# Outputs turned in blocks on VectorE and spread by small DMAs, value products in groups of three key tiles, and a shorter last gate

## What is computed

```python
def _proj(x, w, b, n_head):                 # q, k and v: 8 heads of 16
    y = jax.nn.elu(_conv1d_valid(x, w) + b)
    ...
scores = jnp.einsum('bhqd,bhkd->bhqk', q, k) / jnp.sqrt(jnp.float32(dh))
attn = jax.nn.softmax(scores, axis=-1)
out = jnp.einsum('bhqk,bhkd->bhqd', attn, v)
...
h = _L0_tok_ref(x, ...)
h = h + _L0_attn_ref(_layernorm(h, axis=-1), ...)   # gated unit, one head of 16, causal, gelu
h = h + _L0_ffn_ref(_layernorm(h, axis=-1), ...)    # router with 64 experts, top 2, capacity 128;
                                                    # all experts share w1, b1, w2, b2
```

## Time and profile before

| | us |
|---|---|
| median of 3 runs (824.22 to 829.16) | 825.8 |
| the profiled execution, by its own time | 826.22 |
| its span, from the first to the last instruction | 824.3 |
| PE busy | 793.2 |
| DVE busy | 673.1 |
| ACT busy | 519.8 |
| POOL busy | 259.4 |
| PE's first matmul of the second half, from the start | 538.4 |

### The profile page before, as it was taken

The page is one execution under the profiler, slowest core; times in us unless marked ns, Lnnn a source line. Parts: engine busy times, 40 slices in busy tenths (PEclk is TensorE's granted clock), DMA queues, the critical chain, the costliest instruction groups (busy, mean ns, idle before and its releaser), DMA issues. The chain is left out here.

```text
span 824.3 us, 15525 instructions
## 1 busy us (share of the span) xinstructions
PE 793.2 (96%) x5651; PEld 483.7 (59%) x5651; DVE 673.1 (82%) x1619; ACT 519.8 (63%) x1127; POOL 259.4 (31%) x253
## 2 busy tenths in 40 slices
PE   9799999999999999999999999979999999999996
PEld 5254454454454454454454444447778788787785
DVE  4788889889889889889888989458788887787855
ACT  4067776786786776787687777744645636546432
POOL 3563240350440341341332401314233242342222
PEclk9799999999999999999999999979999999999999
DMA  4462041042042034043032001000000000000001
GB/s 115 70 99 37 1 96 41 1 88 49 1 68 69 1 58 78 1 59 79 1 58 59 2 1 52 1 1 1 1 20 2 20 17 5 20 2 20 20 1 38
DMA packets 32427, 27.92 MB, mean 34 GB/s; under 512 B 5248, under 2 KB 31072, under 8 KB 32352
## 3 DMA queue, kind: packets, MB, share of 16 engines
q1 hardware_dynamic: 32112, 26.64, 16.3%
q10 hardware_dynamic: 240, 0.30, 0.2%
HBM read 4.76 MB, written 3.06 MB: 9 GB/s over the span
## 5 line engine op out<-in xcount | busy, mean ns | idle before, releaser
L429 ACT ACTIVATE probs<-ps_a 128x384 f32<-128x384 f32 (+1 forms) x732 | 299.7, 487 | 76.0 <-PE ps_a L625 71.1
L521 DVE TENSOR_REDUCE neg_max<-ps_a 128x1 f32<-128x512 f32 (+1 forms) x384 | 256.2, 683 | 56.2 <-PE ps_a L641 54.8
L625 PE MATMUL ps_a<-q_rep,k_rep 98*128 98x384 bf16 (+3 forms) x768 | 228.1, 323 | 1.3 <-DVE neg_max L523 1.2
L641 PE MATMUL ps_a<-k_rep,q_rep 96*128 96x512 bf16 (+3 forms) x768 | 219.2, 329 | 6.5 <-DVE neg_max L521 3.5
L641 PEld LDWEIGHTS ps_a<-k_rep,q_rep 96*128 96x128 bf16 (+1 forms) x768 | 76.7, 104 | 109.6 <-DVE neg_max L521 35.3
L656 PE MATMUL ps_pv<-probs,v_hat 128*32 128x364 f32 (+3 forms) x1536 | 140.6, 483 | 0.0
L523 DVE TENSOR_REDUCE neg_max<-ps_a 128x2 f32<-128x472 f32 x192 | 122.9, 640 | 0.0
L625 PEld LDWEIGHTS ps_a<-q_rep,k_rep 98*128 98x128 bf16 (+1 forms) x768 | 79.0, 104 | 58.2 <-ACT probs L429 30.5
L656 PEld LDWEIGHTS ps_pv<-probs,v_hat 128*32 128x32 f32 (+1 forms) x1536 | 40.1, 109 | 64.3 <-issue 58.5
L972 POOL TENSOR_SCALAR rs_v<-mv 128x6 f32<-128x6 f32 x8 | 2.0, 253 | 185.1 <-DVE mv L958 185.1
L258 POOL TENSOR_SCALAR qk_e<-qk_e 128x748 f32<-128x748 f32 x14 | 38.0, 2717 | 29.8 <-ACT qk_e L333 29.8
(11 more groups left out here) (222 smaller groups left out, 1203.0 us busy)
## 6 DMA issues: line engine op xcount, KB each, us to landing
q_rep<-parts_q SPq DMA_DIRECT2D x96, 96.0 KB, 3.8
k_rep<-parts_k SPq DMA_DIRECT2D x93, 96.0 KB, 3.6
xT<-in_x SPq DMA_DIRECT2D x8, 375.0 KB, 4.2
out_h<-y_out SPq DMA_DIRECT2D x7, 320.0 KB
q_rep<-max_T SPq DMA_DIRECT2D x32, 6.0 KB
w_sb<-in_w_T SPq DMA_DIRECT2D x2, 256.0 KB, 3.2
out_h<-y_out SPq DMA_DIRECT2D x8, 54.0 KB
k_rep<-parts_k ACTq DMA_DIRECT2D x3, 96.0 KB, 4.2
```

Source lines behind the costliest of these rows:

```text
L429: act.activation(probs[0:rows(kt), n % RING, 0:w], ps_a[0:rows(kt), 3 + n % 3, 0:w], ACT.Exp, scale=DH ** -0.5).then_inc(p_ready, 1)
L521: dve.tensor_reduce(neg_max[0:rows(t), 0, col:col + 1], ps_a[0:rows(t), c, :], AX.X, ALU.max, negate=True).then_inc(sc_max, 1)
L625: pe.matmul(out[0:rows(kt), 0:QW[qh]], k_rep[0:KM, cb % 2, h, kt * P:kt * P + rows(kt)], q_rep[0:KM, cb % 2, qh, h, 0:QW[qh]], start=True, ...
L641: last = pe.matmul(out, q_rep[0:KS, it % 2, t // QT, h, t % QT * P:t % QT * P + rows(t)], k_rep[0:KS, it % 2, h, 512:L] if c == 2 else k_r ...
```

## The change

- *Outputs.* `copy_output` and `turn_outputs` are gone. DVE's `outputs(cb, i)` turns a quarter straight out of `ps_pv`, in blocks of 32x32 (`dve.transpose`), and takes 12 reciprocals a partition; POOL's new `weigh_outputs` multiplies into `out_n`; SP's new `spread` sends them into `hall` by 16 DMAs for each half of the heads (each 32 partitions x 6 x 16 numbers). Semaphores `spread_done` take the place of `o_done` for those who read `hall`. The statistics of a batch and its `scales` come one iteration later.
- *Values.* `apply_pair` becomes `apply_group`: three key tiles in every third step. `even_step` and `odd_step` become `three_steps`.
- *Places.* What ACT and DVE do beside exponentials and reductions has new places, now given as (step, exponential) and (step, reduction).
- *The end.* For the last batch DVE makes the gates itself (`places_kept`, `gates_last`), the last Gelu comes in two halves, and the output is one fused instruction for a tile.

```diff
@@ first half, SP
+        def spread(cb, g):
+            sp.wait_ge(o_done, cb * 4 + 2 * g + 2)
+            for j in range(GH):
+                for c in range(P // 32):
+                    dst = hall[32 * c:32 * c + 32, cb * LP:(cb + 1) * LP].rearrange("p (t c) -> p t c", c=P)
+                    sp.dma_start(dst[:, :, GH * DH * g + DH * j:GH * DH * g + DH * j + DH],
+                                 out_n[32 * j:32 * j + 32, g, c:BLOCKS:P // 32, :]).then_inc(spread_done[g], 16)
...
                 maxima_rows(it - 1, 3)
+                spread(it - 1, 0)
...
             maxima_rows(it, 2)
+            if it > 0:
+                spread(it - 1, 1)
             if it == B - 1:
                 ahead["load"](sp)
         maxima_rows(B - 1, 3)
+        for g in range(NG):
+            spread(B - 1, g)
@@ first half, POOL
+        def weigh_outputs(cb, i):
+            k, u = cb * 4 + i, i % 2
+            pool.wait_ge(o_inv, k + 1)
...
+            pool.tensor_tensor(out_n[:, i // 2, nb * u:nb * u + nb, :], out_r[:, k % 2, :].rearrange("p (b d) -> p b d", d=32)[:, :, 0:DH],
+                               inv_sum[:, k % 2, :].unsqueeze(2).broadcast_to([P, nb, DH]), ALU.mult).then_inc(o_done, 1)
...
-                for w in "qk":
+            for i, w in enumerate("qk"):
+                if n < B:
                     negative(n, w)
                     residue(n, w)
+                if it > 0:
+                    weigh_outputs(it - 1, 2 + i)
+                if n < B:
                     third_part(n, w)
@@ first half, ACT
-                if s == 6:
-                    middle_part(n, "q")
...
-                if s == 6:
-                    exp_qk(n, "k")
...
+                if at == (5, 3):
+                    exp_qk(n, "k")
+                if at == (8, 0):
                     middle_part(n, "q")
@@ first half, DVE
-                if s == 9:
-                    elu_qk(n, "k")
...
+                if at == (8, 2):
+                    elu_qk(n, "k")
...
+            dve.transpose(out_r[:, k % 2, :], ps_pv[:, 0:QL]).then_inc(pv_copied, 1)
+            dve.wait_ge(pv_copied, k + 1)
+            dve.reciprocal(inv_sum[:, k % 2, :], out_r[:, k % 2, :].rearrange("p (b d) -> p b d", d=32)[:, :, DH]).then_inc(o_inv, 1)
...
+            if at in ((16, 0), (23, 0), (5, 0), (10, 0)):
+                i = ((16, 0), (23, 0), (5, 0), (10, 0)).index(at)
+                if i < 2 or it > 0:
+                    outputs(it - i // 2, i)
@@ first half, PE
+        def apply_group(it, s):
+            p = s - LAG - 3
             cb, cs = (it, p) if p >= 0 else (it - 1, p + STEPS)
...
+            if 0 <= cb < B and cs % 3 == 0:
+                for i in range(3):
+                    apply(cb, cs + i)
@@ second half, the last batch
+            if (n, f) == (B - 1, NF - 1):
+                for h in range(2):
+                    act.activation(hid[:, f, HALF * h:HALF * h + HALF], pair("ffn1", n, f)[:, h, 0:HALF], ACT.Gelu,
+                                   bias=b1_col[:, f:f + 1]).then_inc(S["z_hid"], 1)
...
+        def result_last(n, j):
+            transform(n, j)
+            dve.wait_ge(S["z_yb"], n * 3 + j + 1)
+            for t in range(*PARTS[j]):
+                dve.scalar_tensor_tensor(y_out[:, t, :], y_b[:, t, :], gate[:, t:t + 1], h2[:, n % 2, t, :],
+                                         ALU.mult, ALU.add).then_inc(S["z_out"], 1)
```

More of the change, by code:

```diff
@@ L430, in _ @@
                                            scale=DH ** -0.5).then_inc(p_ready, 1)
-                    if j == 1:
-                        between(it, s)
-                after(it, s)
-        ahead["bias_exp"](act, 1)
+                    after_exp(it, s, j)
         act.activation(warm[:, :], ident[:, 0:1], ACT.Gelu)
@@ L541, in before @@
                 maxima(it, s // 6 - 1)
-            if it == B and s == 0:
+            if at in ((16, 0), (23, 0), (5, 0), (10, 0)):
+                i = ((16, 0), (23, 0), (5, 0), (10, 0)).index(at)
+                if i < 2 or it > 0:
+                    outputs(it - i // 2, i)
+            if it == 0 and c == 1 and s in (2, 4):
+                elu_v(0, (s - 2) // 2)
+            if it > 1 and at in ((18, 0), (20, 2), (21, 0), (21, 1)):
+                part = ((18, 0), (20, 2), (21, 0), (21, 1)).index(at)
+                if part == 0:
+                    for done in spread_done:
+                        dve.wait_ge(done, SPREAD * (it - 1))
+                ahead["statistics"](dve, it - 2, plain_wait, part)
@@ L543, in before, with last @@
+            if it == 1 and at == (13, 0):
+                ahead["bias_sigmoid"](dve, 0)
+            if 2 <= it <= 5 and at in ((13, 0), (15, 0)):
+                ahead["bias_sigmoid"](dve, 2 * it - 3 + s // 15)
+        def last(s):
+            if s == 0:
+                maxima(B - 1, 3)
                 ahead["repeat_weights"](dve)
                 ahead["normalise"](dve, 0)
-            if it > 0 and s - 1 in turns(it):
-                k = turns(it).index(s - 1)
-                outputs(it - 1, k // 2, k % 2)
@@ L584, in _ @@
         copy_qk(1, 0)
-        for it in range(B + 1):
+        for it in range(B):
             for s in range(STEPS):
-                before(it, s)
-                if it < B:
-                    row_max(it, s, 0)
-                between(it, s)
-                if it < B:
-                    row_max(it, s, 1)
-                    row_max(it, s, 2)
+                for c in range(3):
+                    between(it, s, c)
+                    row_max(it, s, c)
+        for s in range(STEPS):
+            last(s)
     @block.tensor
@@ L1580, in _ @@
                     weigh(it, k)
-            if z:
+            if z and it < B:
                 transform(it - 1, 0)
             if it == 0:
+                for done in spread_done:
+                    dve.wait_ge(done, 16 * GH * (P // 32) * B)
                 G["statistics"](dve, B - 1, plain_wait)
@@ L1602, in _ @@
                 sum_2(it)
-        result_last(B - 1)
+        gates_last(B - 1)
+        for j in range(len(PARTS)):
+            result_last(B - 1, j)
     @block.tensor
```

279 lines of the change are left out of this document (138 added, 141 removed).

## The result

The changed kernel takes 868.2 us (median of 4 runs, 866.47 to 869.08) against 825.1 of the kernel before (median of 4). The two medians give a ratio of 1.052; the estimate from all runs is 1.050, with a 95% interval of 1.047 to 1.054. The forecast was 852 with a range up to 866: the sign was right, and the rise too small by 16 us. The profiled execution is the fastest of the four, 866.47 with a span of 864.7, so the spans differ by 40.4 and the medians by 43.1.

The account below looks back on a forecast made before the run. PE was taken to set each batch. Terms 0.5 (first batch) + 15.0 (six batches) + 1.3 (eighth) + 11.2 (boundary) + 1.5 (clock) - 3.1 (end) = +26.4 on 826.2: 852.6, median 852; range 838 to 866.

Parts of the forecast that it names:

- The order that goes wrong: Batches 2 to 7: q's late cast delays POOL's k negative part; DVE's maximum waits 4.4 us; +15.0 us in six.
- Rival 1: Batches 2 to 7: the wait for k's negative part doesn't appear, PE's saving stands; 826 or 819 us; chance 0.16.
- Between the halves: Token attention's end to second half: SP's 16 last transfers hold the barrier, the last group comes later; +11.2 us.
- The clock term: Behind the boundary: one more stretch at half clock after PE idles some 12 us; +1.5 us (0 to 3.4).
- PE's batch without the wait: Token attention, each batch: fewer turning matmuls and groups of three save PE 1.9 us, 63.2 to 61.3.
- The block transposes: DVE, four from PSUM in each batch: 0.55 us each, priced by the nearest PSUM read.
- rival 3: Unknown prices at upper ends, transposes 1.1 us and SP issues 1.26: 870 us and more; chance 0.11 shared with rival 4.
- The eighth batch: No convolutions beside it: groups of three leave DVE as the bound in all eight pieces, 54.5 against 53.2; +1.3 us.
- The end: Last batch: DVE makes gates while PE works, output is one fused instruction a tile; -3.1 us (-2 to -3.5).
- Rival 4: Groups of three starve DVE in batches with convolutions too: +4 us a batch, 875; chance 0.11 shared with rival 3.
- The first batch: Start of token attention: saves a little on PE, waits about 1 us in the same place; +0.5 us.

Follow-up runs that it names:

- pool_order: Changed kernel with POOL making k's negative part ahead of q's third part, ACT's cast of q's middle part staying late: 825.4 us, 0.999 of before.
- filler_17: Changed kernel with 17 useless identity matmuls on PE ahead of the waiting third score of step 9, batches 2 to 7: 853.5 us, 1.034 of before.
- pairs: pool_order with value groups of two key tiles in place of three, two of DVE's outputs also one step later: 854.1 us, 1.035 of before.
- tail_only: Kernel before with only the change's new end (last batch's gates, last Gelu, fused output): 821.3 us against 826.8, 0.994.
- cast_7_1: Changed kernel with ACT's cast of q's middle part moved earlier, behind the second exponential of step 7: 854.8 us, one run.
- cast_6_3: Changed kernel with ACT's cast of q's middle part moved earlier, behind the last exponential of step 6: 853.5 us, one run.
- before_cast_late: Kernel before with ACT's cast of q's middle part moved two steps later, from step 6 to step 8: 834.0 us, one run.
- deferred: pool_order with SP's last 16 transfers to hall issued behind the barrier, as its first work of the second half: 815.3 us, 0.986 of before.
- deferred_loads: deferred with the seven loads of second-half weights ahead of the 16 transfers after the last batch's third rows of maxima: 813.5 us, 0.984 of before.
- filler: Changed kernel with 34 useless identity matmuls on PE ahead of the waiting third score of step 9, batches 2 to 7: 875.1 us, 1.060 of before.

## Why the forecast was too low

**The order that goes wrong** was right in mechanism, place and size. DVE waits 4.6 us and PE 4.2 in each of six batches; the forecast had 4.4. Rival 1, that it doesn't appear, fell. Its upper value, 826, is what pool_order measures, where the cause was taken away.

**The step that failed** is the clock. The prediction gave it a term at one place, behind the boundary, by the earlier trace rows, and none in the six batches, although it forecast there a wait of PE of the same kind and of 4 us. That stretch of before came after four waits of PE of 0.65, 0.67, 0.82 and 1.05 us within ten microseconds (529.2 to 538.4), all shorter than the 4 us forecast for each batch. So the trace of before gave no reason to put the term at nothing there. The kernels pool_order, without the wait, and filler_17, with the wait filled, have no such stretch in their batches. The size: without the wait these six batches take 366.0 us (pool_order) in place of 377.1, -11.0; PE's idle adds 6 x 4.2 = 25.2; of the measured 29.2 that leaves 15.0 for the half clock. In a later batch that is 68.13 - 61.21 - 4.21 = 2.7, and the windows agree: PE works 5.42 us at 0.50, half of which is lost. That is the whole miss of 14.2 in this row of the table; with it the forecast would have been 867.

**Between the halves** it was 13.4 in place of 11.2. From the last value group to PE's first matmul it took 15.35 (566.41 to 581.76) against 5.04 before, +10.3, forecast +9.6. Ahead of the last group it is +3.1, forecast +1.6, and here too the clock can account for the difference, 1.5: it stood at 0.50 from 545.10 to 548.51, after a wait of PE of 1.77 us, and the group at 545.02 took 3.83 us in place of 2.14.

**The clock term** of +1.5 in the second half came to nothing: before, 3.4 and 6.8 us at half clock lay there, 10.2 in all; after, 4.3 at its start and 3.4 later. Expecting one more such stretch was wrong: 9.4 of the 13.7 us at half clock there fell into the long idle, where they cost nothing. Its bound was too high as well: a stretch of 3.4 us at half clock costs at most half its length, 1.7.

**The rest** held in size. PE's batch without the wait: 61.3, measured 61.21. The block transposes: 0.577 (forecast 0.55), so rival 3 fell, with issues at 0.644. The eighth batch: +1.3 and +1.25. The end: -3.1 and -2.9. Rival 4, starving in all batches, fell: DVE waits 3.7 us for scores in a batch of pool_order, against 6.8 before. The eighth batch is right in number only: the forecast had DVE starve behind each group, but it waits 4.0 us for PE's scores there and 4.1 before, and groups of two in pairs did not shorten that batch. What makes its 1.25 is open. The first batch's difference of 0.5 says nothing: its time at half clock differs between executions (13.7 us before, 3.4 after), as in tail_only.

The expected gain of this change did exist: 11.0 us in six batches and 2.9 at the end. The wait behind POOL's queue with its half clock cost 40.2, and the boundary 13.4, of which 10.3 are SP's last 16 issues.

## What to carry to other kernels

When a cast, copy or other small step is moved later on one engine, follow it through every in-order queue behind it: here another tensor's work stood behind it on POOL, and swapping two POOL instructions was worth 43 us. Price a wait of TensorE at its length plus, as the upper bound, the half clock of the work that follows it, wherever the trace of before shows such a stretch behind any idle: here waits of 4.2 us brought it every time, waits of 1.7 to 2.6 us in some places and not in others. Work that only has to be issued, such as small DMAs, belongs behind a barrier, not ahead of it, if its reader waits for its own semaphore anyway; it then delays what stands behind it in the same queue, here by 1.0 us.

## What the runs showed of the hardware

- **The clock can fall after short idles, and need not.** 4.2 us of idle on PE came with 6.83 us at 0.50 in all but the first such batch, which had 3.41; 2.55 us with 3.41 or 6.83 in six of six (cast_7_1); 1.67 us with 3.41 in six of six (cast_6_3); 0.65 us with none (before_cast_late). Against this, 2.64 us ahead of the second half had none behind them in deferred and deferred_loads for 12 us, 2.18 us in the first batch had 6.83 in cast_6_3 and filler but none in the changed kernel and filler_17, and 1.77 us had one in five kernels and none in four. What decides isn't settled. Useless matmuls in the gap of 4.2 us kept the clock at 1.00 and were worth some 15 us.
- **DVE and POOL hold each other up on SBUF.** DVE's instructions over 128x12, 0.16 to 0.17 us elsewhere, took 1.59 and 1.63 when they began just after a 1.6 us instruction of POOL with two inputs in SBUF, and ended with it. The Trainium skill ("SBUF — State Buffer", section "Who interferes with whom") has such a rule: a VectorE instruction with two SBUF inputs and a GpSimd one that reads SBUF share a port pair, and the second to begin waits for the first to end. The first of the two cases is that. The cast at 310.65 has one input and waited as well; the same section lets a cast take the shared pair too, if its operands meet conditions, and no run shows whether this one's did. The cast at 288.65 began beside a POOL instruction of 2.72 and took only 0.74, less than a full wait. No run here separates these cases.
- **Small transfers from SBUF to SBUF cost SP 0.644 us each** in issue at 12 KB, and the replications of 96 KB cost 0.65.
